# Streamed attention with a third slot for stacked keys and queries, row maxima spread over the set, and the sums of probabilities taken by TensorE alone

## What is computed

```python
x = x + tanh(g_xattn[l]) * xattn_l(layernorm(x), ctx)     # l = 0..3
x = x + tanh(g_ffn[l])   * ffn_l(layernorm(x))
```

```python
q, k, v = heads(x @ Wq.T + bq), heads(ctx @ Wk.T + bk), heads(ctx @ Wv.T + bv)
probs = softmax(q @ k.T * 32 ** -0.5)      # layer 1: scores masked and clipped to [-50, 50] first
out = (probs @ v) @ Wo.T + bo
```

## Time and profile before

| | |
|---|---|
| median of 2 runs | 3574.65 us (3563.27 and 3586.04) |
| profiled execution | 3585.96 us, span 3583.9 us |
| granted TensorE clock over the span | 0.868 of full |
| layer 1 attention sets | 857 to 1135 us of the span |
| layer 2 attention sets | 1876 to 2290 us |
| layer 3 attention sets | 2642 to 3066 us |

### The profile page before, as it was taken

One profiled execution on the slowest core, in us unless ns is written; L12 is line 12 of the kernel. 1 busy time (PEld: TensorE's weight loads), 2 busy tenths in 40 slices (PEclk: granted clock), 3 DMA queues, 4 the chain that ended last, 5 costly groups with the idle time before them and its releaser, 6 DMA issues. The chain is left out here.

```text
span 3583.9 us, 34389 instructions
## 1 busy us (share of the span) xinstructions
PE 2802.7 (78%) x10839; PEld 1658.4 (46%) x10839; DVE 1738.8 (49%) x3043; ACT 1189.0 (33%) x2534; POOL 890.7 (25%) x446
## 2 busy tenths in 40 slices
PE   7997998897777618999957676849576677779896
PEld 3554887683222315555522222337432223467663
DVE  3443223675776489898455344421344444334212
ACT  0112111223674259787213232312122333212110
POOL 0001110002884211101006354221234544032112
PEclk9997999897997859999958787969777877889998
DMA  5311533214440000101032312052422221021623
GB/s 200 106 59 49 191 152 126 83 59 96 99 91 7 27 24 24 48 24 47 12 68 53 68 39 59 1 200 83 121 63 61 51 47 33 7 82 53 229 66 108
DMA packets 129004, 269.98 MB, mean 75 GB/s; under 512 B 18768, under 2 KB 46416, under 8 KB 127056
## 3 DMA queue, kind: packets, MB, share of 16 engines
q1 hardware_dynamic: 116368, 227.20, 21.0%
q0 software_dynamic: 12480, 40.90, 3.5%
HBM read 180.49 MB, written 68.42 MB: 69 GB/s over the span
## 5 line engine op out<-in xcount | busy, mean ns | idle before, releaser
L1653 DVE TENSOR_REDUCE L_attn_row_max<-L_attn_rows_ps 128x1 f32<-128x512 f32 x512 | 334.4, 684 | 411.0 <-PE L_attn_rows_ps L1479 408.1
L1633 POOL TENSOR_TENSOR L_attn_total<-L_attn_total,L_attn_probs 128x2048 f32<-128x2048 f32 x105 | 478.3, 4555 | 111.3 <-ACT L_attn_probs L1589 107.8
L1589 ACT ACTIVATE L_attn_probs<-L_attn_s_ps 128x512 f32<-128x512 f32 x512 | 290.5, 597 | 533.6 <-PE L_attn_s_ps L1500 529.2
L1479 PE MATMUL L_attn_rows_ps<-L_attn_k_stack,L_attn_q_stack 96*128 96x512 f32 x512 | 261.8, 542 | 222.1 <-issue 148.8
L437 PE MATMUL L_ffn_hidden<-L_ffn_x_high,L_ffn_up_high 128*128 128x512 f32 x688 | 295.6, 430 | 106.7 <-DVE L_ffn_routes L353 55.2
L1500 PE MATMUL L_attn_s_ps<-L_attn_q_stack,L_attn_k_stack 98*128 98x512 f32 (+1 forms) x768 | 337.7, 503 | 43.2 <-DMA L_attn_q_stack<-L_attn_ml 25.9
L319 ACT ACTIVATE L_ffn_sums<-sims 128x128 f32<-128x128 f32 x1024 | 315.4, 390 | 50.4 <-DVE L_ffn_routes L332 25.9
L1500 PEld LDWEIGHTS L_attn_s_ps<-L_attn_q_stack,L_attn_k_stack 98*128 98x128 f32 (+1 forms) x768 | 155.2, 215 | 297.3 <-issue 134.8
L1479 PEld LDWEIGHTS L_attn_rows_ps<-L_attn_k_stack,L_attn_q_stack 96*128 96x128 f32 x512 | 117.5, 230 | 358.1 <-issue 181.9
L1633 POOL TENSOR_TENSOR L_attn_total<-L_attn_probs 128x2048 f32<-128x2048 f32 x21 | 95.3, 4538 | 725.6 <-ACT L_attn_probs L1589 725.6
L437 PE MATMUL L_ffn_hidden<-L_ffn_x_low,L_ffn_up_high 128*128 128x512 f32 x688 | 273.5, 397 | 0.0
(11 more groups left out here) (284 smaller groups left out, 4680.4 us busy)
## 6 DMA issues: line engine op xcount, KB each, us to landing
L_attn_k_stack<-keys_scratch SPq DMA_DIRECT2D x72, 512.0 KB, 7.0
keys_scratch<-kv_staged SPq DMA_DIRECT2D x48, 512.0 KB, 3.6
L_attn_abs_in<-in_L_ffn_w SPq DMA_DIRECT2D x12, 1024.0 KB, 10.1
values_scratch<-kv_v_sb SPq DMA_DIRECT2D x24, 512.0 KB, 3.4
L_attn_values<-values_scratch SPq DMA_DIRECT2D x24, 512.0 KB, 9.8
L_attn_q_stack<-L_attn_qh SPq DMA_DIRECT2D x192, 64.0 KB, 2.0
L_ffn_xg<-x_slots POOLq DMA_DIRECT2D x46, 256.0 KB, 3.2
y_slots<-L_ffn_y_sb POOLq DMA_DIRECT2D x46, 256.0 KB, 2.3
```

Of the source, the lines that this page charges most:

```text
L1479: nc.tensor.matmul(rows_ps[:, r % R_SLOTS, :], q_stack[0:FOLD, n % 2, h, q * P:(q + 1) * P], k_stack[0:FOLD, n % 2, h, i * HALF:(i + 1) * ...
L1589: nc.scalar.activation(probs[:, g % P_SLOTS, h, :], s_ps[:, v % S_SLOTS, :], ACT.Exp, **kinds).then_inc(exp_done, 1)
L1633: nc.gpsimd.tensor_tensor(total[:], first, probs[:, g % P_SLOTS], ALU.add).then_inc(added, 1)
L1653: nc.vector.tensor_reduce(row_max[:, r // HALVES_K, r % HALVES_K:r % HALVES_K + 1], rows_ps[:, r % R_SLOTS, :], AX_X, ALU.max, negate=True ...
```

## The change

- **A third slot.** `q_stack` and `k_stack` get `SLOTS = 3`. The loads of keys and values are taken out of `stack` into `load(n)`, which is issued for set n+3 behind the last `pv` of set n. `stack(n+2)` is now issued inside set n, ahead of `fold(n+1)`.
- **Rows spread.** `FIRST_ROW` goes from 5 to 1: 32 row products over 26 units instead of 22. The query chunks move from units 12 to 18 to units 9 to 15, the split from 19 and 20 to 16 and 17.
- **Sums.** TensorE sums every group by matmuls with ones, in `pv`, ahead of the product with the values, into a bank of its own, `sums_ps`. GpSimd's additions and `sums` are gone. ScalarE copies the finished sums into `total` (now 128x512) right after `heads_raw`, and VectorE's reciprocals read that. `product_ps` shrinks to one bank.

```diff
-    FIRST_ROW, LAST_ROW, PV_AT = 5, 26, 2
-    CHUNK_AT = {u: (QUERIES, c) for c, u in enumerate((12, 14, 16, 18))}
-    SPLIT_AT, LOW_AT = 19, 20
+    FIRST_ROW, LAST_ROW, PV_AT = 1, 26, 2
+    CHUNK_AT = {u: (QUERIES, c) for c, u in enumerate((9, 11, 13, 15))}
+    SPLIT_AT, LOW_AT = 16, 17
...
                 def stack(n):
-                    s = n % 2
+                    s = n % SLOTS
                     sp.wait_ge(product_free, place[n, QUERIES] + 1)
-                    if n >= 2:
-                        sp.wait_ge(scores_done, UNITS * (n - 1))
+                    if n >= SLOTS:
+                        sp.wait_ge(scores_done, UNITS * (n - SLOTS + 1))
...
-                    if n >= 2:
-                        inputs.load_keys(sp, n)
-                    if n >= 3:
-                        sp.wait_ge(pv_done, KT * (n - 2))
-                    if n >= 2:
-                        inputs.load_values(sp, n)
+                def load(n):
+                    if n >= SLOTS:
+                        sp.wait_ge(scores_done, UNITS * (n - SLOTS + 1))
+                        sp.wait_ge(pv_done, KT * (n - SLOTS + 1))
+                    inputs.load_keys(sp, n)
+                    inputs.load_values(sp, n)
...
+                    if n + AHEAD < SETS:
+                        stack(n + AHEAD)
                     if less_max_rows and n + 1 < SETS:
                         fold(n + 1)
-                    if n + AHEAD < SETS:
-                        stack(n + AHEAD)
+                    if n + SLOTS < SETS:
+                        load(n + SLOTS)
...
                     pe.wait_ge(exp_done, HG * (g + 1))
-                    if g in summed_groups:
...
+                    if kt == 0 and n:
+                        pe.wait_ge(total_taken, n)
+                    for h in range(HG):
+                        last = nc.tensor.matmul(sums_ps[HD * h:HD * (h + 1), :], ones[:], probs[:, g % P_SLOTS, h, :],
+                                                start=(kt == 0), stop=(kt == KT - 1))
+                    last.then_inc(summed, 1)
...
                     nc.scalar.copy(heads[:], o_ps[:]).then_inc(taken, 1)
+                    act.wait_ge(summed, KT * (n + 1))
+                    if n:
+                        act.wait_ge(inverted, n)
+                    nc.scalar.copy(total[:], sums_ps[:]).then_inc(total_taken, 1)
...
-                            nc.gpsimd.tensor_tensor(total[:], first, probs[:, g % P_SLOTS], ALU.add).then_inc(added, 1)
...
-                    last = nc.vector.reciprocal(inv[:, cols], bank(n, SUMS)[:, cols])
+                    last = nc.vector.reciprocal(inv[:, cols], total[:, cols])
```

More of the change, by code:

```diff
@@ L1375, in bank_order @@
             for u in range(UNITS):
-                if u == PV_AT and n and n - 1 not in SUMMED:
-                    order.append((n - 1, SUMS))
                 if u in CHUNK_AT and CHUNK_AT[u][1] == 0 and n + AHEAD < SETS:
@@ L1444, in _ @@
                 stack(1)
+                load(AHEAD)
                 if wo_dram is not None:
@@ L1522, in pv @@
                     for h in range(HG):
[L1523 removed]
+                        last = nc.tensor.matmul(o_ps[HD * h:HD * (h + 1), :], values[:, n % SLOTS, kt, HD * h:HD * (h + 1)],
                                                 probs[:, g % P_SLOTS, h, :], start=(kt == 0), stop=(kt == KT - 1))
                     last.then_inc(pv_done, 1)
[L1527 to L1532 removed]
                 for n, i in FIRST_ITEMS:
@@ L1543, in _ @@
                     for u in range(UNITS):
-                        if u == SUMS_AT and n and n - 1 not in SUMMED:
-                            sums(n - 1)
                         if less_max_rows and u == TURN_AT and n + 1 < SETS:
```

110 lines of the change are left out of this document (38 added, 72 removed).

## The result

The changed kernel takes 3391.95 us, median of 2 runs (3388.67 to 3395.24); before it was 3574.65. The ratio is 0.949 with a 95% interval of 0.935 to 0.963.

A forecast was written before the change was run, and what follows sets the result against it. Sets in layers 2 and 3 stall for their successor's keys; otherwise VectorE's chain bounds them. Layer 1 +41, twelve sets -152, sets 0 +11, ends +4: -96 us, so 3478 us, range 3435 to 3545.

The forecast's parts named there:

- The stall: Layers 2 and 3: six sets a layer wait 12.4 us each for the next set's keys; third slot removes it whole.
- The set rebuilt, "I take 46.0": Layers 2 and 3: a set without its stall, rebuilt two ways, takes 46.0 us instead of 57.8; twelve sets gain 152.
- Rival B: Stall goes, but VectorE's chain takes more, for example with reciprocals and chunks not hidden; sets of 50 us, 3535 us; chance 0.16.
- From 44.3 to 46.0: Layers 2 and 3: set time chosen between 44.3 us, built from groups, and 47.8, built from set 0 of layer 2.
- Layer 1, +41: Layer 1: TensorE's added sums at clock 0.85, copies and later reciprocals cost +41 us, bounds +15 and +60.
- Sets 0 and ends: Layers 2 and 3: set 0's seven more sums, less spread rows, +11 us; set 7 and layer ends +4.
- The rule on the most-contended engine: Skill: optimise the busiest engine first; read plainly, against giving TensorE 126 more sums, which would add 108 us.
- The rule on the clock: Skill: waits between matmul bursts drop the clock, steady load keeps it up; by it sets take 44.3 us, whole 3459.
- set 6 of layer 3: Held against the clock rule: clock 0.62 over 63 us though TensorE is busy 47.24 and only some 13 are stall.
- A: Rival: clock stays up, sums partly hidden; every set at 44.3 us, layer 1 +25, whole 3443 us; chance 0.15.
- C: Rival: slots fail, some other wait holds the row products; residue of 5 us a set, 3539 us; chance 0.07.
- D: Rival: slower, denser sets stay at half clock, some 65 us a set; at share 0.5, 3612 us; chance 0.07.

The follow-up runs named there:

- zeros alone: Kernel of before plus four zero-weight matmuls ahead of the value products of each group GpSimd adds up, GpSimd's additions kept: 3646 us, ratio 1.018.

## Why the prediction was wrong

The direction, the mechanism of the stall and the group times were right; two terms of the sum were mis-sized, the set of layers 2 and 3 and layer 1.

- *The stall.* Right: the third slot removes it whole, and nothing takes its place. By itself it is worth 171 us.
- *The set rebuilt, "I take 46.0".* This step failed; a set takes 41.15 us. The build from groups (44.3) had the new places in it and was right in all but one term: five rows 5.01 (5.08 to 5.15), no rows 3.5 (3.47), change of set 4.4 (4.30). The term that failed is chunks, split and reciprocals, 3.3 + 0.65 + 2.3 = 6.25 us, each priced alone and added in full. 2.8 us were measured, since in the new places chunks and reciprocals fall in the same three groups, the ones on TensorE and the others on VectorE, and hide each other. Rival B named just this pair and had it the other way round, "not hidden at all". The changed kernel with the old places hides less: there a group of six rows takes 5.69 us, and the four groups with chunks or reciprocals are together 4.7 us longer than four of those.
- *From 44.3 to 46.0.* The second build, from set 0 (47.8), pulled the choice up by 1.7 us a set; it too added reciprocals in full, and set 0 has a start with waits.
- *What both come to.* Over the twelve sets 1 to 6 I had 10 x 46.0 + 2 x 42.0 = 544 us; 494.3 were measured. Of the 50 us missed, 32 are the build (3.2 a set in ten sets), 17 the step to 46.0, 1 the sets 6. With the old places the twelve took 539.5 us, and a set at full clock 44.5. That this is near my 544 and 44.3 is chance: I had counted five rows a group. What it does show is that the places are worth 45 us here, which I had put at 0.8 us a set at most.
- *Layer 1, +41.* This failed too: +10.5. The group of 3.96 us was right to the hundredth. Wrong were two things. At full clock eight groups take 34.25 us (1011.88 to 1046.13) where they took 30.95, so 3.3 us a set are felt, with ScalarE's second copy and the chunks' new places in it, and not 5.5: I had taken half-clock prices for part of the sums, and in the groups with chunks a sum is hidden in part. And I kept the clock at 0.85, where the added matmuls raise it to 0.96 (0.98 with zeros alone). 2.2 us in seven sets are 15, so by this estimate each of the two is about half of the 30 us missed.
- *Sets 0 and ends.* +11 was +8.7; the +4 for the ends cannot be told apart from the rest, which came out 7.3 us shorter.
- *The rule on the most-contended engine* would have added 108 us for the sums. Measured are 38 to 55 for all three layers (3408 to 3446, 3337 to 3392, 3578 to 3633). It was right that they are not free: the change without them is the faster one.
- *The rule on the clock.* The Trainium skill, page "TensorE: Matmul & The Clock Gate", section "HAM oscillation — how this bites in real kernels", says that steady work keeps the clock up. I held set 6 of layer 3 against it. In the changed kernel the trace agrees with the rule: 1.00 through whole sets of layer 2, and zeros in the gaps of layer 1 raised 0.86 to 0.98. Set 6 had a stall at its start, so it was no evidence against it; why its clock stayed down behind the stall, as that of layer 2's sets did not, is open.
- *Rivals.* A (clock stays up, 3443) was the right one in kind, and still 51 us too slow: it took the 44.3 of the build, and +25 for layer 1. B, C and D are out: the chain did not take more, no wait remained, and the clock went up, not down.

Of the 94 us between forecast and measurement (190.4 less 96), 50 are the twelve sets, 30 layer 1, and 14 sets 0, the ends and what is spread over the other blocks.
